# Two-layer cross-attention on one core: where VectorE makes the third block's low part in the first layer, and where TensorE uses it

## What is computed

```python
text, ip = ctx[:, :77, :], ctx[:, 77:, :]
q = split_heads(x @ Wq.T)
out  = merge(softmax(q @ split_heads(text @ Wk.T).T * D**-0.5) @ split_heads(text @ Wv.T))
out += merge(softmax(q @ split_heads(ip @ Wk_ip.T).T * D**-0.5) @ split_heads(ip @ Wv_ip.T))
x1 = out @ Wo.T + bo + x
```

## Time and profile before

| | us |
|---|---|
| median of 3 runs | 1678.19 |
| lowest and highest of them | 1675.7, 1682.73 |
| the profiled execution | 1678.24 |
| its span, from the first to the last instruction | 1676.4 |

### The profile page before, as it was taken

One profiled execution on the slowest core, in us unless ns is written; L12 is line 12 of the kernel. 1 busy time (PEld: TensorE's weight loads), 2 busy tenths in 40 slices (PEclk: granted clock), 3 DMA queues, 4 the chain that ended last, 5 costly groups with the idle time before them and its releaser, 6 DMA issues.

```text
span 1676.4 us, 25931 instructions
## 1 busy us (share of the span) xinstructions
PE 1580.9 (94%) x7968; PEld 1190.7 (71%) x7968; DVE 1280.6 (76%) x3552; ACT 1096.5 (65%) x2323; POOL 560.3 (33%) x1313
## 2 busy tenths in 40 slices
PE   6899999999999999999999999999999999999993
PEld 3565489999456459999756537999965654899981
DVE  3698279898789538899779835999887982798985
ACT  1697278886388537888438926888726872788860
POOL 0243034443044214444214403444403430344430
PEclk9899999999999999999999999999999999999995
DMA  9010310010311221001121122000030113000100
GB/s 316 22 44 16 113 56 25 20 36 1 114 34 39 78 69 54 20 20 31 51 73 40 45 90 75 20 21 24 22 113 23 41 31 113 15 25 20 36 1 16
DMA packets 65953, 83.90 MB, mean 50 GB/s; under 512 B 29188, under 2 KB 36628, under 8 KB 65816
## 3 DMA queue, kind: packets, MB, share of 16 engines
q1 hardware_dynamic: 63144, 77.11, 15.6%
q10 hardware_dynamic: 2672, 5.13, 0.9%
HBM read 41.49 MB, written 34.10 MB: 45 GB/s over the span
## 4 chain that ended last, share of the span: by engine, by line
PE 75%; DVE 10%; ACT 8%; issue 3%; DMA 1%; SPq 1%; POOL 1%; POOLq 0%; ACTq 0%; DVEq 0%
PE ps_w L1006 41%; PE ps_s L1006 16%; PE ps_t L1006 11%; PE ps_b L1006 5%; ACT probs L577 3%; DVE probsT_low L758 3%; DVE row_max L822 2%; PE ps_b L1140 2%; ACT probsT_high L558 2%; ACT probsT L566 2%; DVE probs L846 1%; DVE stat L831 1%; ACT probs L592 1%; PE ps_m L1006 1%; DMA slots<-out_all 1%
## 5 line engine op out<-in xcount | busy, mean ns | idle before, releaser
L558 ACT ACTIVATE probsT_high<-ps_t 128x512 fp32r<-128x512 f32 x640 | 384.3, 600 | 101.6 <-PE ps_t L1006 101.5
L758 DVE TENSOR_TENSOR probsT_low<-probsT,probsT_high 128x512 fp32r<-128x512 f32 x560 | 385.0, 688 | 39.4 <-ACT probsT L566 34.6
L566 ACT ACTIVATE probsT<-ps_t 128x512 f32<-128x512 f32 x640 | 387.2, 605 | 0.0
L1006 PE MATMUL ps_w<-gram,probsT_high 128*128 128x416 f32 (+2 forms) x1280 | 383.1, 310 | 0.0
L1006 PE MATMUL ps_w<-gram_low,probsT_high 128*128 128x384 f32 (+2 forms) x1280 | 352.1, 304 | 0.0
L485 POOL TENSOR_SCALAR exp_bias<-row_max 128x1 f32<-128x1 f32 x320 | 136.8, 428 | 544.7 <-DVE row_max L822 544.7
L592 ACT ACTIVATE probs<-ps_s,exp_bias 128x508 f32<-128x508 f32 x320 | 220.9, 691 | 130.6 <-POOL exp_bias L485 89.6
L1006 PE MATMUL ps_s<-slots 96*128 96x512 f32 x640 | 281.1, 481 | 21.2 <-DVE row_max L773 9.7
L1006 PE MATMUL ps_t<-slots 98*128 98x512 f32 x640 | 252.2, 415 | 1.8 <-ACT probsT L566 1.4
L1006 PEld LDWEIGHTS ps_w<-gram_low,probsT_high 128*128 128x128 f32 (+1 forms) x1280 | 242.0, 189 | 6.5
L1006 PE MATMUL ps_w<-gram,probsT_low 128*128 128x400 f32 (+2 forms) x1280 | 246.1, 314 | 0.0
(11 more groups left out here) (168 smaller groups left out, 2100.9 us busy)
## 6 DMA issues: line engine op xcount, KB each, us to landing
slots<-parts SPq DMA_DIRECT2D x128, 192.0 KB, 3.3
parts<-probsT_high SPq DMA_DIRECT2D x16, 512.0 KB, 4.0
parts<-probsT_high SPq DMA_DIRECT2D x24, 256.0 KB, 3.7
parts<-probsT_low SPq DMA_DIRECT2D x8, 512.0 KB, 3.4
parts<-x_sb SPq DMA_DIRECT2D x8, 512.0 KB, 3.9
slots<-probsT_high SPq DMA_DIRECT2D x24, 128.0 KB, 3.3
parts<-probsT_low SPq DMA_DIRECT2D x12, 256.0 KB, 3.6
ctx_sb<-in_ctxT ACTq DMA_DIRECT2D x3, 1024.0 KB, 5.5
```

Of the source, the lines that this page charges most:

```text
L558: nc.scalar.activation(probsT_high[1 - par][:, t, :], ps_t[:, t % 2, :], ACT.Exp, scale=SCALE)
L566: nc.scalar.activation(probsT[:, t, :], ps_t[:, t % 2, :], ACT.Exp, scale=SCALE).then_inc(pt_block[l], 1)
L758: nc.vector.tensor_tensor(probsT_low[1 - par][:, t, :], probsT[:, t, :], probsT_high[1 - par][:, t, :].bitcast(F32), ALU.subtract).then_in ...
L1006: return nc.tensor.matmul(out, lhsT, rhs, start=start, stop=stop)
```

## The change

In VectorE's `step0`, the low part of block 2 is made in the next step, between maxima A and lowT 0 (that step calls it with the numbers of the step before, `n - 1` and `1 - par`). In TensorE's `step0`, `values_low(2)` moves from ahead of scores B to behind it. No instruction is added or removed, and none of ScalarE, GpSimd or SyncE moves.

```diff
@@ VectorE, step0
                 if scores:
                     maxima0(b, n + 2, 1, par)
+                if use:
+                    lowT(b, 0, n - 1, 1 - par, 2)
                 if first:
                     maxima0(b, 1, 0, 1)
...
                                             axis=AX.X, op=ALU.add).then_inc(o_moved, 1)
-                if transposed:
-                    lowT(b, 0, n, par, 2)
@@ TensorE, step0
                 if use:
                     values_low(0)
                     values_low(1)
-                    values_low(2)
                 if scores_next and not first:
                     scores_half(3, 0)
                 if use:
+                    values_low(2)
                     values_low(3).then_inc(oT_done, 1)
```

## The result

| | before | after |
|---|---|---|
| median of 17 runs, us | 1680.11 | 1683.74 |
| lowest and highest, us | 1674.95, 1682.73 | 1680.56, 1687.03 |
| the profiled execution and its span, us | 1678.24, 1676.4 | 1681.8, 1680.0 |

The ratio of after to before is 1.0023, with a 95% interval of 1.0014 to 1.0032: 2.4 to 5.4 us slower. The prediction said 1686.0 us against 1678.2, so +7.8, no difference that counts as one, with 1677 to 1695 as its range. Sign and class came out as forecast, the size at half.

What follows compares the result with a forecast made beforehand. VectorE and the two score banks were taken to set the 5.12 us step; a held lowT 2 makes it 5.22. Per batch .06 + 1.50 + .38 = 1.94, 7.8 for four, on 1678.2: 1686.0 us, range 1677 to 1695.

Steps and rivals of the forecast that it cites:

- Sign and class: Whole program: slower by 7.8 us, just below the 8.4 us that counts as a difference; same .49, slower .39, faster .12.
- What bounds the kernel: First layer's full step: a loop through VectorE and the two score banks sets the 5.12 us.
- crowded half: VectorE between maxima B and next maxima A: three operations in a row while scores A wait; the move frees about .5 us.
- The hold: VectorE's lowT 2 meeting GpSimd's running subtraction is held until that ends, then needs another .55 us.
- The new loop: lowT 2, values_low 2, values_low 3, copy, exponentials, GpSimd, back to lowT 2: 5.22 us a step, .10 more.
- Rival 1: VectorE's lowT 2 is not held; the loop from scoresT 0 takes 4.88 us, total 1662; chance .12.
- The first and the last distance: Between L805s in each batch: first full step .06 us longer, step 16 to 17 .38 longer (4.88 against 4.50).
- The sum for the first layers: Touched L805 distances: .06, 15 times .10 and .38 make 1.94 us a batch, 7.8 for four.
- Cost of GpSimd's value slots: GpSimd part meeting a running VectorE part: none counted, as lowT 1 would be over by 2.41.
- the .09 that I had worked out as spare: VectorE in the new loop: lowT 1 and L805 leave it free at 2.68, maxima A start at 2.77.
- Rival 3: After release lowT 2 runs its whole .68 us: loop 5.35, .13 more, total 1695; chance .06.

Runs made afterwards that it cites:

- the two ways of emptying its crowded half without a hold: Changed kernel, GpSimd and VectorE swapping low parts of blocks 2 and 3: 1658.14 us; kernel before, L805 moved between next step's maxima, values_low 2 behind scores B: 1666.65 us.
- run with fills: Changed kernel with GpSimd's low-part subtraction of block 3 replaced by two zero fills of the same tile: 1663.88 us; the same edit in the kernel before: 1677.2 us.
- the shortened one: Changed kernel with GpSimd's low-part subtraction of block 3 cut to 448 of 512 columns: 1670.87 us in one run, 1676.67 for the kernel before beside it.

## Why the prediction came out as it did

- **What bounds the kernel.** Right. VectorE's loop of 5.12 stood in all three profiles of before and in the run with TensorE's half alone, and the two ways of emptying its crowded half without a hold brought the step to 4.89 and 4.96.
- **The hold.** Right: four overlaps in the last steps of the layer, each with an end .54 or .55 behind GpSimd's, were the evidence. After the change it was .56 in a full step, and L758 took 1.26 against the forecast 1.25. The run with fills removed it without touching the order.
- **The new loop.** Right link by link: 5.22 forecast, 5.22 measured (83.5 / 16). Rival 1 (not held, 4.88) would have been right by its size: it is the kernel with fills, at 4.89.
- **The first and the last distance.** .06 and .38 forecast. In the first profile after, the last distance was 4.83 to 4.88 against 4.50, so .33 to .38. The first was 5.38, 5.22, 5.10 and 5.22 in the four batches against 5.12, and 5.59 and 5.61 in batch 0 of the other two profiles: the .06 is right in no batch. The errors are small in the sum and partly cancel.
- **The sum for the first layers.** 7.8 forecast, 7.4 to 7.6 measured in three profiles against three.
- **The term that was off** is one that the sum did not have, for the rest of the program: "the profiled execution took 1678.24 ... and is as good as the median". The sum took what lies outside the first layer as fixed. It was 4.1 us shorter, mean of three against three, which is over half of the forecast difference, and this goes with TensorE's higher granted clock. So the loops were right, and that the medians lie only 3.6 us apart was not foreseen; the range covered it, with 1683.74 well inside.
- **Cost of GpSimd's value slots.** I counted none for lowT 1. It takes .73 instead of .68 (1312.48): GpSimd's two casts for the value slots end at 1312.66 and lowT 1 at 1313.21, again .55 behind. Before the change lowT 1 began only .09 ahead of the casts' end, which costs nothing. It lies off the loop and cost nothing: the next maxima A start .38 behind the reduction (1313.13 to 1313.51), where back to back it is .35, so .03 of the .09 that I had worked out as spare was left.
- **Rival 3** (the whole .68 after the release) is excluded: .54 to .56 behind GpSimd's end wherever VectorE's subtraction was lengthened by GpSimd's, in every kernel that shows it.

The page "SBUF — State Buffer" of the Trainium skill, in "Who interferes with whom", says that a VectorE instruction with two SBUF inputs contends with a GpSimd instruction that reads SBUF and not with one that only writes it. The traces agree: 1.26 behind a subtraction and .68 beside two fills. The page calls the shared ports an exclusive lock; its words that the other one fully blocks stand with VectorE's two-port modes. Here the held subtraction ended .55 behind the other's end, less than its own .68, so part of its time passes under the hold.

## What to carry to other kernels

Before you move an instruction into a gap of its engine, look at what the other engines do in that gap, GpSimd above all if both subtract two SBUF operands; a few overlaps elsewhere in the same trace, if only at the ends of a loop, price it. Then write the loop that the delay closes, not only the delay: here the hold added .58 to VectorE, the move freed .5 in its crowded half, and what counted was that the engine that held it waited, two engines further on, for the held one. And if the loop runs through the other engine's start time, ask whether that engine can take the part that is ready earlier: this turned +0.2% into -1.3%, of which 1.0% lies in the first layers. And a forecast for one stretch is checked on that stretch: here what lies outside it moved the total by half as much as the change did.

## What the runs showed of the hardware

GpSimd held VectorE up with no semaphore between the two, so the engines do not meet at semaphores alone. A VectorE subtraction of 128x512 that began while GpSimd's was running ended .54 to .56 us behind GpSimd's end, while a free one takes .68: with overlaps of .37, .57, .61 and .70 it took .92, 1.12, 1.15 and 1.26, with .14 or less .68 to .70. GpSimd's own took 1.28 to 1.30 in these cases (1.16 the shortened one). VectorE's reductions out of PSUM were not lengthened beside it (.43 and 1.05). GpSimd's two casts took .84 instead of .37 where VectorE's subtraction began between their starts. Two GpSimd fills of 128x512 took .53 each and neither held VectorE nor were held. TensorE's granted clock in the last 45 us of the program, which the change does not touch, was 0.61 in three profiles of one kernel and 0.66 to 0.73 in three of the other; I had not expected that and can't explain it.
